# A generator that yields between quantizing a weight chunk and transposing it, beside an attention loop

## The reference, cut to what matters

```python
x = x + ga * attn(layernorm(x) * (1 + ca) + sa)      # 8 heads of 128, causal, T = 2048
h = layernorm(x) * (1 + cb) + sb
x = x + gb * ffn(h)                                  # 1024 -> 2816 -> 1024, SiLU gate

def fp4_linear(x, w):                                # the FFN's three products
    return fp4_quant_dequant(x) @ fp4_quant_dequant(w).T
# fp4_quant_dequant: blocks of 16 along the last dim; scale = max|x| / 6;
# every |x| / scale goes to the nearest of 0, .5, 1, 1.5, 2, 3, 4, 6; times scale
```

## Time and profile before

| what | value |
|---|---|
| median of 3 runs | 11181.06 us (11174.88 to 11181.25) |
| profiled execution, its own time | 11181.55 us |
| its span on the slowest core (core 6) | 11180.0 us |
| spans of the eight cores | 11145.2 to 11180.0 us |
| PE / DVE / ACT busy | 51% / 62% / 10% of the span |
| mean granted TensorE clock, core 6 | 0.716 of full |
| attention loops of sequences 0 to 3 begin at | 1042, 2692, 3977, 5070 us |
| transposes of chunks (L393) | first at 1060.2 us, last at 3023.9 us |
| FFN | from about 5750 us on |

### The profile page before, as it was taken

One profiled execution on the slowest core, in us unless ns is written; L12 is line 12 of the kernel. 1 busy time (PEld: TensorE's weight loads), 2 busy tenths in 40 slices (PEclk: granted clock), 3 DMA queues, 4 the chain that ended last, 5 costly groups with the idle time before them and its releaser, 6 DMA issues.

```text
span 11180.0 us, 79969 instructions; the slowest of 8 cores (11145.2 to 11180.0 us)
## 1 busy us (share of the span) xinstructions
PE 5718.6 (51%) x21080; PEld 2175.2 (19%) x21080; DVE 6913.6 (62%) x16690; ACT 1099.8 (10%) x2066; POOL 125.7 (1%) x167
## 2 busy tenths in 40 slices
PE   1044345444474668456845545545555455545545
PEld 0021111121121222122212222222222222212222
DVE  6764655455624432443247777777777777777777
ACT  0000011100131013101300000000000000000000
POOL 0000000000000000000000000000000000000000
PEclk5577666677686878687867777677777777767777
DMA  3112111121101100111020000000000000000000
GB/s 72 48 34 26 32 28 30 39 32 24 30 31 49 19 24 30 49 19 35 19 83 12 16 12 12 12 16 12 12 14 14 12 12 16 10 14 12 15 12 12
DMA packets 202414, 278.61 MB, mean 25 GB/s; under 512 B 106796, under 2 KB 142252, under 8 KB 200952
## 3 DMA queue, kind: packets, MB, share of 16 engines
q1 hardware_dynamic: 78152, 214.21, 5.7%
q0 software_dynamic: 123824, 59.29, 4.4%
HBM read 248.23 MB, written 84.51 MB: 30 GB/s over the span
## 4 chain that ended last, share of the span: by engine, by line
DVE 44%; PE 28%; DVEq 12%; issue 7%; DMA 7%; ACT 2%; POOL 1%; SPq 0%; ACTq 0%; POOLq 0%
DVEq L91 12%; PE pG L1028 3%; PE pG L692 2%; PE pG L819 2%; DMA xt<-xmid_scr 2%; PE pA L770 2%; PE pA L671 2%; PE pG L800 2%; PE pD L795 2%; DVE qd_g_f L498 2%; PE pEF L800 2%; PE pH L1008 2%; PE pC L795 2%; DVE qd_q_f L498 2%; DVE qd_q_f L524 2%
## 5 line engine op out<-in xcount | busy, mean ns | idle before, releaser
L955 PE MATMUL pA<-wgT,xqf 128*128 128x512 bf16 x1536 | 658.7, 429 | 1203.9 <-DVE hmid L987 998.6
L1028 PE MATMUL pG<-wdT,hqf 128*128 128x512 bf16 x2816 | 1044.4, 550 | 173.4 <-DVE hqf L1013 173.4
L1008 PE MATMUL pH<-identb,hq_t 128*128 128x128 bf16 x1408 | 180.5, 306 | 1189.8 <-DVEq L995 1189.8
L740 DVE COPY recipb<-pG 128x512 f32<-128x512 f32 x128 | 88.6, 692 | 999.7 <-PE pG L734 999.7
L791 ACT ACTIVATE union<-pA 128x512 bf16<-128x512 f32 (+1 forms) x640 | 354.9, 555 | 3570.2 <-PE pA L776 2056.1
L961 PE MATMUL pC<-wuT,xqf 128*128 128x512 bf16 x1536 | 657.1, 428 | 0.0
L955 PE MATMUL pB<-wgT,xqf 128*128 128x512 bf16 (+1 forms) x1536 | 594.6, 387 | 0.0
L961 PE MATMUL pD<-wuT,xqf 128*128 128x512 bf16 (+1 forms) x1536 | 588.0, 383 | 0.0
L1028 PEld LDWEIGHTS pG<-wdT,hqf 128*128 128x128 bf16 x2816 | 352.6, 130 | 807.1 <-issue 745.3
L671 PE MATMUL pA<-union,wbuf 128*128 128x512 bf16 x1024 | 316.6, 465 | 287.6 <-DVE stag L677 107.1
L955 PEld LDWEIGHTS pA<-wgT,xqf 128*128 128x128 bf16 x1536 | 163.9, 107 | 1404.7 <-issue 1319.8
(11 more groups left out here) (169 smaller groups left out, 10882.4 us busy)
## 6 DMA issues: line engine op xcount, KB each, us to landing
xt<-x SPq DMA_DIRECT2D x128, 512.0 KB, 3.9
xmid_scr<-xw SPq DMA_DIRECT2D x64, 512.0 KB, 2.9
xt<-xmid_scr SPq DMA_DIRECT2D x64, 512.0 KB, 4.2
out<-xw SPq DMA_DIRECT2D x64, 512.0 KB, 2.9
wmb<-wmod POOLq DMA_DIRECT2D x12, 1024.0 KB, 10.7
wbuf<-wq POOLq DMA_DIRECT2D x32, 256.0 KB, 5.3
wbuf<-wk POOLq DMA_DIRECT2D x32, 256.0 KB, 5.6
wbuf<-wv POOLq DMA_DIRECT2D x32, 256.0 KB, 6.0
```

What stands on the lines that cost most here:

```text
L955: self.op('T', lambda E, cc=c, o=io, w=iw, p=pGt: E.matmul(p[:, 0:w], self.xqf[:, cc, :], self.wgT[:, cc, o:o + w], start=(cc == 0), stop= ...
L1008: self.op('T', lambda E, cc=c, k2=kk, hq=hqt[i]: E.transpose(pH[:, k2, :], hq[:, cc * 128:(cc + 1) * 128], self.identb[:]), chT if kk == n ...
L1028: st=(ib == 0 and c == 0), sp=lastd: E.matmul(pG[:, ha * 512:(ha + 1) * 512], self.hqf[:, k2, :], self.wdT[:, ig, ha * 512:(ha + 1) * 512] ...
```

## The change

The generator yields once more, between the marker behind the quantization and TensorE's wait for it. The value of VectorE's counter is kept in `qmark` before that, since other code raises the counter in between. So a chunk takes two calls instead of one.

```diff
             self._emit_qd([(buf[:, 0:512], buf[:, 0:512], 512)])
             self._emit_qd([(buf[:, 512:1024], buf[:, 512:1024], 512)])
             self.op('V', lambda E: E.engine_nop(), chV)
-            self.wait('T', chV, chV.n)
+            qmark = chV.n
+            yield
+            self.wait('T', chV, qmark)
             self.waitm('T', self.r_pH.guard())
             for hc in range(8):
                 self.op('T', lambda E, b_=buf, hh=hc: E.transpose(
```

## The result

The changed kernel takes 10848.32 us (median of 8 runs, 10833.46 to 10875.64) where the kernel before takes 11174.23 (8 runs, 11160.69 to 11181.25). The ratio is 0.9712, 95% interval [0.9701, 0.9723]: 322 us less, between 310 and 334 (the two medians are 326 apart). The forecast was 10848, with a range from 10765 to 10905; the time measured lies in it.

A forecast was written before the change was run, and what follows sets the result against it. TensorE idled 751.7 us before the transposes, waiting for VectorE's quantization, with nothing overlapping. Gains of 311.9 (blocks), 19.7 (gaps) and 1.4 (first block) sum to 333 us, taking 11181 to 10848; range 10765 to 10905.

The forecast's parts named there:

- The odd head runs beside the quantization: Attention slots after a quantization: TensorE no longer waits before the transposes, so the odd head overlaps VectorE's work; blocks gain 311.9 us.
- VectorE's chain of 24.3 us: Odd L740-to-L740 interval: copy and product 1.47, quantization 16.54, 0.3, then reciprocal to next L740 5.98; longest plain interval 19.5.
- The reciprocal behind the quantization is what is late next: VectorE's in-order queue: the even head's reciprocal L726, 3.35 us, follows the quantization, and TensorE's broadcast L734 waits for it.
- Even intervals stay plain, with transposes in the stall: Even intervals keep plain length P: eight transposes, 0.8 us, fit in TensorE's 1.88 us stall; 26 us if that cover were gone.
- The sum: Whole kernel: 311.9 us from blocks, 19.7 from gaps and 1.4 from the first block make 333 us gained.
- the 17.5 us of a slot: Slots with a chunk before the change: quantization and transposes together take 17.5 us, from 1069.14 to 1086.83 less 0.2.
- L397 adds 0.8 in slot 7: Last slot of a block: no head follows, the second reciprocal comes at once, so VectorE's copy L397 adds 0.8 to 7.7 us.
- slot 0 takes 22.8 us: Block start: from the last addition L834 to the first L740, 22.8 us with quantization, against plain 13.7 or 20.9.
- Gaps between blocks: From L740 of head 7 to the next block's head 0: 57.7, 59.6, 63.2 us after; 19.7 us gained altogether.
- Spreading over 44 more slots costs 107.6 us in sequence 2 (blocks): Sequence 2, blocks 0 to 2, formerly without chunks, lengthen by 46.7, 35.7 and 25.2 us, 107.6 together.
- No stretch of VectorE beside busy engines: Quantization beside a busy TensorE and ScalarE: zero lengthening taken; a tenth on 16.3 us would cost 65 us.
- Even heads could start at the fast clock: Rival for even heads: transposes fill the stall, saving 2 us x 33 = 66 us, time 10780; chance 0.06.

## Why the prediction was right, point by point

- *The odd head runs beside the quantization, and VectorE's chain of 24.3 us sets the interval in every block.* Shown: 23.7 to 24.5, on average 24.1, in the 33 odd intervals of the profile after; with half the quantization some 8 less; with the broadcast taken out of the chain 21.6.
- *The reciprocal behind the quantization is what is late next.* Shown by TensorE's wait of 15.41 us at the broadcast. But moving it forward wins only the broadcast, 2.4 us, not its own 3.35.
- *Even intervals stay plain, with transposes in the stall.* Right in length. One reason was incomplete: the transposes were on the path before, some 0.7 to 1.1 us a slot, as the kernel before without quantization shows. The sum had it, inside the 17.5 us of a slot, and it came out right.
- *L397 adds 0.8 in slot 7; slot 0 takes 22.8 us.* The interval in slot 7 is 8.4 (1164.2 to 1172.6) against 7.7, so 0.7 to 0.8. Gaps between blocks were 57.9, 58.6 and 66.4 in sequence 0 against 57.7, 59.6, 63.2; the last is over by 3, which no run explains. As the mean of eight cores all gaps together gave 12.4 us where the sum had 19.7. On the other hand the stretches from one sequence's last block to the next one's first were 10 us shorter, where the sum had nothing. No run explains these either; the two misses cancel.
- *Spreading over 44 more slots costs 107.6 us in sequence 2 (blocks).* Right within 3 us by the block lengths, and shown from the other side by placing fewer chunks in the short blocks: 0.9712 to 0.9575.
- *No stretch of VectorE beside busy engines.* Over all 352 chunks of the eight cores the quantization took 16.19 us on average, and 16.21 before. The one shown above took 16.48 (1074.53 to 1091.01), with a pause of 0.42 ahead of one instruction, and that in the earlier trace rows 16.32.
- *Even heads could start at the fast clock; given 0.06.* In the changed kernel they do not: eight transposes left 0.91 us idle, and in the first 6 us of these heads the mean granted clock was 0.55 over eight cores, as forecast. Twenty-five transposes left none, and it was 0.88. So the mechanism exists, but it takes more than the change gives. The argument against it, that in a chunk slot of before transposes directly ahead of the head did not help, compared heads behind a pause of 17 us with only eight transposes ahead of them. The price given, 2 us a head or 66 us, was too high: the even intervals gave some 26 us for 33 heads, 0.8 us each.

The blocks carry the forecast: 309 us less as the mean of eight cores, with 312 forecast. That the forecast met the median by 0.3 us is luck: the changed kernel's own runs range over 42 us, the misses in the gaps and between the sequences cancel, and the sum started from 11181, where the later median of the kernel before is 11174.

## What to carry to other kernels

When work for another stage is slipped into a pipelined loop, the wait between its parts and not the work itself can be the cost: emit the consumer's wait one step later than the producer's work, and the consumer's in-order queue gets to the next step's work while the producer is still busy. What remains is then, for each step, the longer of two queues, and could here be added up from one profile. So halve and place the pieces until the queue with the added work is no longer than the step, and keep them out of a step that nothing follows. Look again at every other wait once pieces sit closer: the wait for the store, which never held anything up in the changed kernel, took some 3.5 us a time as soon as the slots were packed.

## What the runs showed of the hardware that was not expected

What TensorE does between the broadcast and the next head changes the clock granted to that head. Behind the broadcast, eight transposes and 0.91 us idle, a matmul of the head shown took 0.58 us; behind the broadcast and twenty-five transposes without a pause it took 0.38. This is one run, and it changes two things at once, the pause and the amount of TensorE's work ahead of the head; which of them does it was not tested, nor whether filling the stall in all 128 slots would win more. The pause alone does not decide. In the same trace a head starts at the full level behind a stall of 1.88 us and falls back within two matmuls, core 4:

```profile
3871.26 0.38 PE L776 MATMUL pA<-q_fm,k_fm 128*128 128x512 bf16 x1 [1.88 <-DVE union L749]
...
3872.48 0.58 PE L801 MATMUL pD<-union,v_tm 128*128 128x512 bf16 x1 [0.62 <-ACT union L797]
```

And in the kernel before, 292 of 296 heads that follow eight transposes at once start at the half level, behind the pause for the quantization. The Trainium skill ("TensorE: Matmul & The Clock Gate", Loop structure matters more than you think) says that VectorE's copy does not break warmth where the next matmuls follow immediately. The traces here agree only in part: with the stall filled the mean granted clock of the head's first 6 us was 0.88, but 145 of the 264 heads still began at the half level; behind the plain stall of 1.88 us it was 0.59.

Besides 0.5 and 1.0 a third granted clock, 0.81, appears in stretches of up to 51 us. In seven of the fourteen profiled executions it is on the cores of one die alone (cores 0 to 3, or 4 to 7), in the other seven on both. In the kernel before without quantization, core 0, a stretch of attention and for comparison the length of its matmuls:

```profile
1344.50:1354.40 9.90, 9.26 (x32) 2.57 (x30) 0.39 (x1) 4.14 (x8) 0.00 (x0) 0.81 0.00 0
```

```profile
1344.44 0.44 PE L793 MATMUL pD<-union,v_tm 128*128 128x512 bf16 x1
1344.81 0.42 PE L798 MATMUL pG<-union,ones_c 128*1 128x512 bf16 x1
```

A 512-column matmul takes 0.42 to 0.44 there, against 0.38 at the full clock and 0.59 at half. The medians of the two dies in that run were 10499.5 and 10464.0 us, with mean clocks of 0.717 and 0.735; only the first die has this clock, 1103 to 1303 us of it on each core. In the changed kernel without quantization cores 2 and 3 had some 860 us of it between their first and last L742 and took 10494.9 and 10465.4 us, cores 0 and 1 none and 10431.7 and 10443.8; but cores 6 and 7 had 496 us of it there too and took 10416.9 and 10431.3. So it is argued, not shown, to be part of the 31 and 56 us by which the runs without quantization exceeded the sum.
